# Cross-attention and quantised feed-forward on one core: paired result stores, the mean weight in the row scales, step sizes on GpSimd, 352 columns to GpSimd

## The reference

```python
h = layernorm(x, ln1_g, ln1_b)
h = bitlinear(h, w1, b1)              # 256 -> 1024
h = gelu(h)
h = layernorm(h, ln2_g, ln2_b)        # over the 1024 columns
h = bitlinear(h, w2, b2)              # 1024 -> 256
x = x + h

def bitlinear(x, w, b):
    dqx = round(x * s) / s            # s = 127 / max(|x|, 1e-5), one per row
    dqw = clip(round(w * v), -1, 1) / v   # v = 1 / mean(|w|)
    return dqx @ dqw.T + b
```

## Time and profile before

| | us |
|---|---|
| median of 3 runs | 1011.82 (1011.65 to 1012.08) |
| the profiled execution | 1012.12 |
| its span | 1010.4 |
| ACT busy | 932.4 (92%) |
| PE busy | 926.0 (92%) |
| DVE busy | 906.2 (90%) |
| POOL busy | 783.4 (78%) |

### The profile page before, as it was taken

How to read it: one execution, slowest core, us unless ns; L and a number is a source line. 1 busy time by engine, 2 the same in 40 slices (tenths; PEclk the granted TensorE clock), 3 DMA queues, 4 the chain that set the end, 5 groups by cost and what they waited for, 6 DMA issues and landing times.

```text
span 1010.4 us, 26145 instructions
## 1 busy us (share of the span) xinstructions
PE 926.0 (92%) x7519; PEld 568.6 (56%) x7552; DVE 906.2 (90%) x1193; ACT 932.4 (92%) x2642; POOL 783.4 (78%) x1188
## 2 busy tenths in 40 slices
PE   9999999999999999999999888888888888888887
PEld 7666666666666666666666533344444444444435
DVE  3688888888888888888888899999999999999997
ACT  5789999999999999999998789999999999999996
POOL 2476666787667666677767588999999999999996
PEclk9999999999999999999999969999999999999999
DMA  5668887777786666666586425878878777777785
GB/s 154 166 183 191 182 181 160 167 171 156 154 167 170 172 168 169 171 164 167 159 162 146 114 64 83 127 132 126 126 126 126 126 126 126 126 126 126 127 127 94
DMA packets 243888, 146.74 MB, mean 145 GB/s; under 512 B 183896, under 2 KB 201816, under 8 KB 243824
## 3 DMA queue, kind: packets, MB, share of 16 engines
q1 hardware_dynamic: 234176, 129.03, 58.5%
q0 software_dynamic: 8640, 15.73, 12.2%
q10 hardware_dynamic: 1008, 1.18, 0.3%
HBM read 71.36 MB, written 33.63 MB: 104 GB/s over the span
## 4 chain that ended last, share of the span: by engine, by line
PE 56%; POOL 17%; issue 14%; DVE 6%; ACT 5%; POOLq 1%; DMA 0%; ACTq 0%; DVEq 0%
PE banks L1460 11%; PE banks L1446 10%; POOL nq L624 7%; PE banks L1362 6%; PE banks L1417 6%; PE banks L1406 5%; PE banks L1437 4%; POOL out L615 3%; POOL g_rq L652 3%; PE banks L1427 3%; POOL gn_high L641 2%; PE banks L1395 2%; PE banks L1431 2%; PE banks L1287 2%; DVE gn_low L877 1%
## 5 line engine op out<-in xcount | busy, mean ns | idle before, releaser
L1287 PE MATMUL banks<-w_t,h_t 128*128 128x512 bf16 x472 | 126.4, 388 | 70.3 <-DVE gn_low L877 34.9
L791 DVE TRANSPOSE_TENSOR_REDUCE nm_part<-banks 128x64 f16<-128x2048 f32 x64 | 147.6, 2307 | 0.9 <-PE banks L1362 0.7
L1083 ACT ACTIVATE probs<-banks 120x512 f32<-120x512 f32 x256 | 132.3, 602 | 14.9 <-PE banks L1395 11.4
L1144 ACT ACTIVATE g_dev<-banks,g_sum 128x1024 bf16<-128x1024 f32 x128 | 144.0, 1125 | 0.0
L1138 ACT ACTIVATE banks<-banks,h_dq 128x1024 f32<-128x1024 f32 x128 | 140.3, 1096 | 3.8 <-PE banks L1292 3.7
L1460 PE MATMUL banks<-wo_sb,o_t 128*128 128x256 f32 x512 | 135.2, 399 | 1.9 <-DVE xr L797 1.3
L1316 PE MATMUL banks<-w_t,g_t 128*128 128x256 bf16 x1024 | 133.6, 274 | 1.8 <-ACT g_t L1164 1.8
L1316 PEld LDWEIGHTS banks<-w_t,g_t 128*128 128x128 f16 x1024 | 90.2, 98 | 61.4 <-issue 51.5
L1446 PE MATMUL banks<-xt,wq_c 128*128 128x256 f32 x512 | 121.5, 380 | 0.0
L1287 PEld LDWEIGHTS banks<-w_t,h_t 128*128 (+1 forms) x504 | 48.0, 98 | 121.2 <-issue 90.6
L1460 PEld LDWEIGHTS banks<-wo_sb,o_t 128*128 128x128 f32 x512 | 87.1, 190 | 37.5 <-ACT log_sum L1072 25.4
(11 more groups left out here) (177 smaller groups left out, 2516.5 us busy)
## 6 DMA issues: line engine op xcount, KB each, us to landing
x_in<-in_x SPq DMA_DIRECT2D x64, 256.0 KB, 3.7
xt<-in_x_t SPq DMA_DIRECT2D x64, 256.0 KB, 5.1
xr<-in_x SPq DMA_DIRECT2D x64, 256.0 KB, 5.1
out<-xr SPq DMA_DIRECT2D x64, 256.0 KB, 5.3
out<-h POOLq DMA_DIRECT2D x60, 256.0 KB, 4.9
ctx_t<-in_ctx_t SPq DMA_DIRECT2D x64, 128.0 KB, 4.8
r_bc<-r_rows SPq DMA_DIRECT2D x61, 128.0 KB, 4.8
w_raw<-in_w_t SPq DMA_DIRECT2D x8, 256.0 KB, 5.4
```

The costliest lines, as they stand in the source:

```text
L791: dve.tensor_reduce(nm_part[:, :, 0:C * RB], blocks_p, AX.X, ALU.max, negate=True, apply_transpose=True).then_inc(max_done, 1)
L1083: act.activation(probs[:, p, j, :, :], sc_p[0:KV, j, :, :], ACT.Exp, scale=SCALE).then_inc(probs_done, 1)
L1144: act.activation(g_dev[:, t, :], u_p[t], ACT.Square, scale=-float(F), bias=g_sum[:, p, t:t + 1], accum_out=g_ssq[:, p, t:t + 1]).then_inc( ...
L1287: pe.matmul(u_p[t][:, cols], h_t[:, b, t * C + c, :], w1_t[:, c, cols], start=(c == 0), stop=False, skip_group_check=True)
```

## The change

Five edits, all in one diff:

- PART grows from 304 to 352 columns.
- POOL issues one store for two batches (`store_pair`, 512 KB) in every second pass; there are two semaphores `stored` instead of four.
- `step_size` moves from ACT to POOL, as a multiplication with a constant tile of 1/127 ahead of `scales`. Its output in `g_vm`, now with four slots, also serves ACT as the scale of the result; `out_scale` and `g_dq` go, save for the last batch.
- The mean weight m goes into the row scales: the scale of the squares and epsilon are divided by m squared (`ve_mul`, `ve_add`), the floor of the maximum is 1e-5 times m, and the affine offset is spread over the partitions by a row of m instead of ones. The five values are formed once, by DVE, in `scale_by_mean`.
- POOL's waits of `quantise_batch` stand ahead of the second `gain_part` (`quantise_waits`).

```diff
-    PART = 304
+    PART = 352
...
-        g_vm = sb("g_vm", [P, 2, 2 * T])
+        g_vm = sb("g_vm", [P, 4, 2 * T])
...
+                pool.memset(inv_qmax[:, :], 1.0 / QMAX).then_inc(powers_set, 1)
...
-                def store(b, r):
-                    pool.wait_ge(out_done, b * T + T)
-                    pool.dma_start(out[b].rearrange("(p t) n -> p t n", p=P), res[:, r, :, :],
-                                   accum_op=ALU.add).then_inc(stored[r], 16)
-
-                def out_scale(b, r):
-                    pool.tensor_tensor(g_dq[:, r, :], g_max[:, r, :], w_out[:, 0:1].to_broadcast([P, T]),
-                                       ALU.mult).then_inc(gdq_done, 1)
+                def store_pair(b, m):
+                    pool.wait_ge(out_done, (b + 1) * T + T)
+                    pool.dma_start(out[bass.ds(b, 2)].rearrange("b (p t) n -> p b t n", p=P), res[:, 2 * m:2 * m + 2, :, :],
+                                   accum_op=ALU.add).then_inc(stored[m], 16)
...
-                def quantise_batch(b, r):
+                def quantise_waits(b, r):
                     pool.wait_ge(gr_done, b + 3)
...
+                def step_size(b, r):
+                    after(pool, gr_done, b + 1)
+                    after(pool, out_done, (b - 4) * T + T)
+                    pool.wait_ge(g_maxed, b + 1)
+                    pool.tensor_tensor(g_vm[:, (r + 2) % 4, T:2 * T], g_max[:, r, :], inv_qmax[:, :], ALU.mult).then_inc(gmx_done, 1)
...
                 def ffn(j, n):
                     gain_part(j, 0, n)
                     b = j - 6
-                    if live(b, NB):
-                        store(b, (n + 2) % 4)
-                    scales(j, n % 2)
+                    if n % 2 == 1 and live(b, NB):
+                        store_pair(b - 1, ((n + 2) % 4) // 2)
+                    step_size(j - 2, (n + 2) % 4)
+                    scales(j, n)
+                    quantise_waits(j - 2, (n + 2) % 4)
                     gain_part(j, 1, n)
                     quantise_batch(j - 2, (n + 2) % 4)
...
+                def scale_by_mean():
+                    dve.wait_ge(mean_done, 2)
+                    dve.tensor_scalar(w_floor[:, :], w_mean[:, 1:2], CLIP, None, ALU.mult).then_inc(mean_done, 1)
+                    dve.tensor_scalar(w_row[:, :], ones[0:1, :], w_mean[0:1, 1:2], None, ALU.mult).then_inc(mean_done, 1)
+                    dve.tensor_tensor(w_inv2[:, :], w_inv[:, 1:2], w_inv[:, 1:2], ALU.mult).then_inc(mean_done, 1)
+                    dve.wait_ge(mean_done, 5)
+                    dve.tensor_scalar(ve_mul[:, :], w_inv2[:, :], 1.0 / F ** 3, None, ALU.mult).then_inc(mean_done, 1)
+                    dve.tensor_scalar(ve_add[:, :], w_inv2[:, :], LN_EPS, None, ALU.mult).then_inc(mean_done, 1)
...
-                        dve.memset(gn_floor[n], CLIP).then_inc(floor_set, 1)
+                        dve.wait_ge(mean_done, 3)
+                        dve.tensor_copy(gn_floor[n], w_floor[:, :].unsqueeze(1).to_broadcast([P, T, 1])).then_inc(floor_set, 1)
...
-                def step_size(b, r):
-                    after(act, gr_done, b + 1)
-                    act.wait_ge(g_maxed, b + 1)
-                    act.activation(g_vm[:, r % 2, T:2 * T], g_max[:, r, :], ACT.Copy, scale=1.0 / QMAX).then_inc(gmx_done, 1)
+                    act.activation(g_vm[:, n, 0:T], g_ssq[:, p, :], ACT.Identity, scale=ve_mul[:, 0:1], bias=ve_add[:, 0:1]).then_inc(gve_done, 1)
...
-                    act.activation(res[:, r, t, :], y2_tiles[t], ACT.Copy, scale=g_dq[:, r, t:t + 1]).then_inc(out_done, 1)
+                    act.activation(res[:, r, t, :], y2_tiles[t], ACT.Copy, scale=g_vm[:, (r + 2) % 4, T + t:T + t + 1]).then_inc(out_done, 1)
...
-                        last = pe.matmul(bank[t][:, :], ones[0:1, :], b2n_bc[0:1, t * 512:(t + 1) * 512],
+                        last = pe.matmul(bank[t][:, :], w_row[:, :], b2n_bc[0:1, t * 512:(t + 1) * 512],
```

More of the change, by code:

```diff
@@ L231, in xattn_ffn @@
         g_ssq = sb("g_ssq", [P, 2, T])
-        g_vm = sb("g_vm", [P, 2, 2 * T])
+        g_vm = sb("g_vm", [P, 4, 2 * T])
+        ve_mul = sb("ve_mul", [P, 1])
+        ve_add = sb("ve_add", [P, 1])
+        w_floor = sb("w_floor", [P, 1])
+        w_inv2 = sb("w_inv2", [P, 1])
+        w_row = sb("w_row", [1, P])
+        inv_qmax = sb("inv_qmax", [P, T])
         g_rq = sb("g_rq", [P, 2, 2 * T])
@@ L272, in xattn_ffn @@
         out_done = sem("out_done")
-        stored = [sem(f"stored{r}") for r in range(4)]
+        stored = [sem(f"stored{m}") for m in range(2)]
         last_max = sem("last_max")
@@ L642, in gain_part, with scales @@
                                        g2_bc[:, F - PART:F], ALU.mult).then_inc(part_done, 1)
+                def step_size(b, r):
[3 more added lines that the diff above has]
+                    pool.tensor_tensor(g_vm[:, (r + 2) % 4, T:2 * T], g_max[:, r, :], inv_qmax[:, :], ALU.mult).then_inc(gmx_done, 1)
                 def first_scales(b):
                     pool.wait_ge(gve_done, b + 1)
-                    pool.tensor_tensor(g_rq[:, b % 2, 0:T], g_vm[:, b % 2, 0:T], powers[:, 0:T], ALU.pow).then_inc(gr_done, 1)
-                def scales(b, p):
+                    pool.tensor_tensor(g_rq[:, b % 2, 0:T], g_vm[:, b, 0:T], powers[:, 0:T], ALU.pow).then_inc(gr_done, 1)
+                def scales(b, n):
                     pool.wait_ge(g_affine, (b - 1) * T)
@@ L700, in _ @@
                 add_b2(NB - 1, 3)
-                scales(2, 0)
+                step_size(0, 0)
+                scales(2, 2)
+                quantise_waits(0, 0)
                 gain_part(2, 1, 2)
@@ L714, in _ @@
                 steps(pool, 4, NB, FFN_L0, FFN_L1, ffn, 4, {4: lambda: split_scales(2), 5: first_parts_stored})
+                step_size(NB - 2, 2)
                 last_scales()
+                quantise_waits(NB - 2, 2)
                 quantise_batch(NB - 2, 2)
-                store(NB - 6, 2)
-                store(NB - 5, 3)
+                store_pair(NB - 6, 1)
                 pool.wait_ge(last_quant, 1)
-                out_scale(NB - 1, 3)
+                last_out_scale()
                 for b, r in ((NB - 4, 0), (NB - 3, 1)):
@@ L723, in _ @@
                     pool.tensor_tensor(xr[:, r, :, :], xr[:, r, :, :], res[:, r, :, :], ALU.add).then_inc(late_sum, 1)
-                for r in range(4):
-                    pool.wait_ge(stored[r], NB * 4 - 16)
+                for m in range(2):
+                    pool.wait_ge(stored[m], NB * 4 - 16)
             @block.vector
@@ L899, in largest_rows @@
                         dve.wait_ge(floor_set, j + 1)
-                    after(dve, gdq_done, j - 3)
+                    after(dve, gmx_done, j - 3)
                     dve.wait_ge(g_affine, j * T + T)
@@ L987, in _, with add_residual @@
                 dve.tensor_scalar(nq[:, 1, 1, :], gn[3][:, 1, :], last_scale[:, 1:2], HALF_ONE, ALU.mult, ALU.add).then_inc(last_quant, 1)
-                def add_residual(b, t, r, y):
-                    dve.scalar_tensor_tensor(out=xr[:, r, t, :], in0=y[t], scalar=g_dq[:, r, t:t + 1],
+                def add_residual(b, t, r, y, scale):
+                    dve.scalar_tensor_tensor(out=xr[:, r, t, :], in0=y[t], scalar=scale[:, t:t + 1],
                                              in1=xr[:, r, t, :], op0=ALU.mult, op1=ALU.add).then_inc(last_out, 1)
@@ L994, in _ @@
                 dve.wait_ge(x1_stored[2], NB * 4)
[L995 removed]
+                dve.wait_ge(gmx_done, NB - 1)
                 for t in range(T):
                     dve.wait_ge(y2_ps, (NB - 2) * T + t + 1)
[L998 removed]
+                    add_residual(NB - 2, t, 2, y2_first, g_vm[:, 0, T:2 * T])
                 dve.wait_ge(x1_stored[3], NB * 4)
+                dve.wait_ge(gdq_done, 1)
                 for t in range(T):
                     dve.wait_ge(last_y, t + 1)
[L1002 removed]
+                    add_residual(NB - 1, t, 3, y2_tiles, last_dq)
             @block.scalar
@@ L1149, in deviation, with variance @@
                                    bias=g_nm[:, p, t:t + 1]).then_inc(part_centred, 1)
-                def variance(b, p):
+                def variance(b, p, n):
                     after(act, gr_done, b - 1)
+                    if isinstance(b, int) and b == 0:
+                        act.wait_ge(mean_done, 7)
                     act.wait_ge(ssq_done, b * T + T)
-                    act.activation(g_vm[:, p, 0:T], g_ssq[:, p, :], ACT.Copy, scale=1.0 / F ** 3, bias=LN_EPS).then_inc(gve_done, 1)
-                def step_size(b, r):
-                    after(act, gr_done, b + 1)
-                    act.wait_ge(g_maxed, b + 1)
-                    act.activation(g_vm[:, r % 2, T:2 * T], g_max[:, r, :], ACT.Copy, scale=1.0 / QMAX).then_inc(gmx_done, 1)
+                    act.activation(g_vm[:, n, 0:T], g_ssq[:, p, :], ACT.Identity, scale=ve_mul[:, 0:1], bias=ve_add[:, 0:1]).then_inc(gve_done, 1)
                 def gelus_turned(b):
@@ L1167, in residual @@
```

(11 more changed lines are left out.)

20 lines of the change are left out of this document (8 added, 12 removed).

## The result

The changed kernel takes 1026.9 us (median of 4 runs, 1026.0 to 1029.1) against 1011.7 (4 runs of before, 1011.6 to 1012.1): the ratio is 1.0144, 95% interval 1.0123 to 1.0165. It is wrong in sign and outside the range.

A forecast was written before the change was run, and what follows sets the result against it. VectorE was taken as the bound at 6.346 us a pass, ScalarE and GpSimd close behind; passes at ScalarE's 6.27 save 4.0 and 0.7, with -0.2 at the end and +0.3 for mean weight: 1007.4 us, range 1005.5 to 1019.

The forecast's parts named there:

- Columns: Second part, 48 more columns to GpSimd, twice a pass: VectorE falls 0.10 us, ScalarE gains 0.08, GpSimd gains 0.21.
- I take nothing for it, with 0 to +0.04 as bounds: ScalarE's variance with scale and offset from SBUF: no added cost, since `part` already has such an operand.
- GpSimd's own waits: GpSimd's pass, power waiting for step size and gain for power: 0.07 to 0.08 us each; pass 5.69 without the store.
- The dearer value, 5.85: GpSimd's pass without the store, in us, if two further waits behind the power each cost as much again.
- The pair store: GpSimd's 512 KB store every second pass: 0.98 us in two passes taken, up to 1.1; bounds 0.98 and 1.91.
- break-even of 1.31: Pair-store cost in us at which GpSimd's two passes equal today's 12.69; above it the kernel is slower than today.
- the two citations in the prediction: Skill passages on GpSimd's DMA: many descriptors before incremental cost shows; recorded end at last descriptor written, speaking for growth with rows.
- Mean weight: First part, five tiny VectorE operations for one: 0.8 us at most, 0.3 taken, counting on slack between VectorE and TensorE.
- The end: Kernel's end: step size no longer passes through ScalarE, one store issue goes; -0.2 us, bounds 0 and -0.5.
- Rival A: The pair store costs by its rows and GpSimd becomes the bound: 1018 to about 1030 us; chance 25%.
- B: Gain eaten by GpSimd's new chain of own waits or a pair store of 1.2 to 1.35: 1010 to 1013; chance 20%.
- The signs that the prediction set: Pair store under 1.15 us: forecast stands; over 1.3: wrong. Power over 0.35 after step size, or gain over 0.2 after power: B.

The follow-up runs named there:

- b_vm: Kernel before with only the variance changed: scale and offset from SBUF (constants), Identity instead of Copy; 1021.0 us, ratio 1.0100.
- b_mean: Kernel before with only the five small VectorE operations of scale_by_mean added in pass 20, results unread; 1015.1 us, ratio 1.0036.
- a_port: Kernel after, with the squared inverse as a one-input VectorE operation and the row of 128 formed by ScalarE in a later pass; 1021.2 us, ratio 1.0095.
- g_352: The change with 352 columns, step size first on GpSimd, immediates in the variance, mean weight multiplied once into the gain by GpSimd; 1012.35 us, ratio 1.0010.
- h_336: Kernel before plus pair stores, step size first on GpSimd, 336 columns; quantisations' wait for the power behind the second gain; 1007.9 us, ratio 0.9965.

## Why the prediction was wrong

The method held: a pass costs what its busiest engine spends, and with the measured terms the sum comes out. GpSimd's 6.52 against 6.346 over 60 passes is +10.4, the first part +6.4: 1012.1 + 16.8 = 1028.9, and the profiled execution took 1029.1. This is a check made afterwards, on one execution. The terms failed, five of them, all in one direction. (The sum on record also has a slip: 4.0 + 0.7 + 0.2 - 0.3 is 4.6, not 4.4, so its own terms give 1007.2.)

- *Columns: right.* VectorE's centring takes 0.83 (predicted 0.88 - 0.05), `part` 0.44 (0.44), the first gain 0.89 (0.88), GpSimd +0.19 (+0.21).
- *"I take nothing for it, with 0 to +0.04 as bounds": the step that failed on ScalarE.* The variance costs +0.18 to +0.19 a pass. I argued from `part`, which has one SBUF operand; the variance has two, where it had none. The Trainium skill, "ScalarE: Activation LUTs" (what ACT_TABLE_LOAD costs), gives about 93 ns for each `[128,1]` pointer operand, by my estimate from it 186 for two; the trace agrees (the first variance takes 0.38 us in the kernel after, 0.20 before). ScalarE: 6.24 became 6.42, with the turn of the loop, which rose too (0.20 over the usual instead of 0.12), 6.46. By itself this is the +9 us of b_vm.
- *GpSimd's own waits: the cheap end was taken.* The pass without a store is 5.91 against 5.69. From the step size to the power it is 0.34 (I had 0.27), from the power to the gain 1.25 (1.11), and 1.02 to the quantisation as predicted. The chain of the earlier trace rows runs between instructions of 0.20; behind the power a wait costs 0.24 more than a plain succession (1.25 against 1.01). The dearer value, 5.85, was in the text and is nearer. The wait behind the power came in with the fifth edit, of which the prediction weighed only the wait for the turned buffer; its cost stood under the step size. No run has the kernel after with this one wait moved back.
- *The pair store: 0.98 taken, 1.22 measured* (7.13 - 5.91). Its instruction lasts 1.26 against 0.93. Under my break-even of 1.31, and harmless alone, but added to the waits it makes 12.36 into 13.04: 0.44 from the waits, 0.24 from the store. The cost isn't at the store: the next instruction starts 0.84 behind it, and the rest is mostly the wait for the step size, 0.80 instead of 0.34. On the two citations in the prediction: the Trainium skill, "DMA: Bandwidth & Descriptors", has the incremental cost of descriptors show up late, but here 128 more rows cost 0.33 us, and the measurement decides, though two thirds of the 0.93 don't grow. The Trainium skill, "Perfetto Trace Analysis", puts the recorded end at the last descriptor written, and the growth agrees with that.
- *Mean weight: "0.8 at most" was 6.* I counted five instructions at the 0.15 of the earlier trace rows, a `tensor_scalar` of one column. GpSimd was busy there too (two quantisations, from 996.52 to 998.85 in the trace of before), so a quiet GpSimd isn't why it was cheap. What differs is the form: two of the five had another, and took 1.23 and 1.27. Slack between VectorE and TensorE, on which I relied, was not there: no later pass makes the delay good. Of the 6 us, 2.5 are the two instructions themselves (b_mean); a_port, where neither takes that form on VectorE, gets 5.7 back. The step of 1.9 us at pass 31, where VectorE waits 2.3 us for the DMA of `r_bc`, is 0.8 in b_mean and 0.6 in a_port; why it is larger in the kernel after is open.
- *The end: -0.2 was +3.8.* The lag of GpSimd, hidden by buffers for 60 passes, is paid when they are empty. It is part of the +10.4 above (6.9 between the variances, 3.8 behind them), not a further term.

Rival A named the right engine and the right sign for another price; B named the own waits, with too little weight and no sum with A; neither stood beside a ScalarE above the old pace. The two were treated as alternatives, but they are terms of one sum with 0.18 us of cover in two passes. The signs that the prediction set point at B: the gain starts 0.24 after the power's end (over 0.2), the power 0.34 after the step size (just under 0.35), and the pair store's 1.26 lies between its two marks. Yet B's price, 1010 to 1013, was 14 us too low.

## What to carry to other kernels

When three engines stand within 0.1 us of each other, sum each engine's new pass at the dear end of every unknown before looking at the cheap one; here each of three "free" edits was more than the cover. Price an instruction by its form (number of SBUF inputs, of scalars from SBUF) and by what runs beside it, not by its size. Work that GpSimd must issue in order pays for each wait on itself, so put something between a producer and its reader, and when waits are moved as a group, ask what each of them now holds up.

## What the runs showed of the hardware

- A VectorE instruction on 128x1 with two SBUF inputs took 1.23 us, and a `tensor_scalar` on 1x128 took 1.27, while GpSimd added 512 columns; the one-input form of the first took 0.20.
- A ScalarE instruction on 128x2 with scale and offset from SBUF (b_vm) costs 0.28 to the next start against 0.10 with immediates.
- A recorded duration on ScalarE isn't its cost. In b_vm `part` lasts 0.66 and the next starts 0.40 after its start, as before, where it lasted 0.52.
- Behind a store, GpSimd's next instructions overlap it and are recorded longer (power 1.34 to 1.49 instead of 1.01). The time comes due at the first instruction that waits for their result (1.75 from the power to the gain in g_352), or at the quantisation (0.73 behind the result scale in h_336 instead of 0.29).
